# Retention attention and a mixture of experts on one core: score steps taken five at a time in place of two, and values read in another order

## The reference, cut to what matters

```python
s = jnp.einsum('bthd,bshd->bhts', q, k) * scale
logits = DEG * jnp.log(jnp.abs(s) + 1e-30) + log_G[:, :, :, None] - log_G[:, :, None, :]
logits = jnp.where(mask, logits, -jnp.inf)
m = jax.lax.stop_gradient(jnp.max(logits, axis=-1, keepdims=True))
a = jnp.exp(logits - m)
num = jnp.einsum('bhts,bshd->bthd', a, v)
den = jnp.sum(a, axis=-1).transpose(0, 2, 1)
y = num / (den[..., None] + 1e-06)      # then a norm over 64 columns, times ln_w, times w_proj
```

## Time and profile before

| | us |
|---|---|
| median of 3 runs (lowest, highest) | 1057.96 (1056.93, 1059.55) |
| the profiled execution, its own time | 1058.96 |
| its span, first to last instruction | 1056.9 |
| PE busy | 994.3 (94%) |
| DVE busy | 874.1 (83%) |
| ACT busy | 670.4 (63%) |
| POOL busy | 606.8 (57%) |

### The profile page before, as it was taken

The page is one execution under the profiler, slowest core; times in us unless marked ns, Lnnn a source line. Parts: engine busy times, 40 slices in busy tenths (PEclk is TensorE's granted clock), DMA queues, the critical chain, the costliest instruction groups (busy, mean ns, idle before and its releaser), DMA issues.

```text
span 1056.9 us, 23328 instructions
## 1 busy us (share of the span) xinstructions
PE 994.3 (94%) x8871; PEld 684.2 (65%) x8871; DVE 874.1 (83%) x1730; ACT 670.4 (63%) x1077; POOL 606.8 (57%) x593
## 2 busy tenths in 40 slices
PE   4999989999998999999999999999999999999884
PEld 2675565666665767676767676767676676767563
DVE  5678748898989998988998879898888899889972
ACT  1342445766666677777677868676878766776551
POOL 0311538888897565565756374756475666557421
PEclk9999999999999999999999999999999999999896
DMA  9301214443433353543544353545253335445530
GB/s 259 95 2 46 55 52 110 109 98 96 104 101 97 99 147 83 134 98 83 123 123 119 98 136 83 121 107 139 71 129 89 88 98 138 101 91 126 137 106 21
DMA packets 77951, 108.65 MB, mean 103 GB/s; under 512 B 15853, under 2 KB 46445, under 8 KB 77712
## 3 DMA queue, kind: packets, MB, share of 16 engines
q1 hardware_dynamic: 72768, 104.50, 38.8%
q0 software_dynamic: 5072, 2.67, 1.9%
HBM read 31.61 MB, written 11.36 MB: 41 GB/s over the span
## 4 chain that ended last, share of the span: by engine, by line
PE 74%; DVE 11%; POOL 4%; DMA 4%; issue 3%; ACT 2%; SPq 2%; POOLq 0%; DVEq 0%; ACTq 0%
PE PS L713 20%; PE PS L521 19%; PE PS L742 18%; PE PS L516 6%; PE PS L564 2%; PE PS L567 2%; PE PS L574 2%; DVE PS L1304 2%; DMA U<-H_d 2%; POOL U L1407 1%; SPq L461 1%; POOL xe_d L1439 1%; POOL Kt L1410 1%; DVE U L1271 1%; PE PS L537 1%
## 5 line engine op out<-in xcount | busy, mean ns | idle before, releaser
L713 PE MATMUL PS<-Qt,Kt 64*128 64x256 f32 (+1 forms) x2560 | 295.4, 370 | 8.1 <-DVE U L1271 7.1
L713 PEld LDWEIGHTS PS<-Qt,Kt 64*128 64x128 f32 x2560 | 219.6, 187 | 81.4 <-issue 51.7
L742 PE MATMUL PS<-U 128*64 128x256 f32 (+1 forms) x1792 | 191.6, 354 | 11.4 <-ACT U L899 11.4
L888 ACT ACTIVATE U<-PS 128x1024 f32<-128x1024 f32 x192 | 188.2, 1016 | 11.1 <-PE PS L713 8.1
L884 ACT ACTIVATE U<-U 128x768 f32<-128x768 f32 x128 | 107.7, 841 | 113.1 <-DVE U L1271 112.9
L742 PEld LDWEIGHTS PS<-U 128*64 128x64 f32 x1792 | 121.6, 138 | 87.6 <-issue 32.1
L1407 POOL TENSOR_TENSOR U<-U,consts 128x512 f32<-128x512 f32 x96 | 125.1, 1303 | 88.7 <-DMA U<-U 88.7
L1304 DVE SCALAR_TENSOR_TENSOR PS<-U,ES,PS 128x512 f32<-128x512 f32 x192 | 144.8, 754 | 17.7 <-ACT U L888 8.7
L1271 DVE SCALAR_TENSOR_TENSOR U<-PS,U 128x768 f32<-128x768 f32 x128 | 119.5, 953 | 42.6 <-PE PS L713 35.5
L1429 POOL TENSOR_SCALAR_AFFINE_SELECT U<-U 128x256 f32<-128x256 f32 x128 | 70.0, 547 | 105.4 <-ACT U L812 104.8
L1475 POOL TENSOR_TENSOR U<-U,SM 128x1024 f32<-128x1024 f32 x32 | 61.0, 1906 | 77.6 <-DVE SM L1324 77.5
(11 more groups left out here) (163 smaller groups left out, 1542.1 us busy)
## 6 DMA issues: line engine op xcount, KB each, us to landing
G<-U SPq DMA_DIRECT2D x512, 64.0 KB
U<-U SPq DMA_DIRECT2D x192, 128.0 KB, 2.4
U<-H_d SPq DMA_DIRECT2D x32, 512.0 KB
Kt<-Kt SPq DMA_DIRECT2D x32, 256.0 KB, 3.8
U<-in_w SPq DMA_DIRECT2D x21, 256.0 KB
acc<-in_x SPq DMA_DIRECT2D x4, 512.0 KB, 5.6
ye_d<-G SPq DMA_DIRECT2D x4, 512.0 KB, 8.3
U<-ye_d SPq DMA_DIRECT2D x4, 512.0 KB, 5.2
```

Of the source, the lines that this page charges most:

```text
L713: mm = te.matmul(bank[:, 256 * n:256 * n + 256 - lo], Kt[u % 2][(ki + hd) % 2][rows, 128 * j:128 * j + 128], Qt[p % 2][m // 2][rows, 256 * ...
L742: mm = te.matmul(P[4][64 * hd:64 * hd + 64, c + lo:c + 256], vt, A[s % NA][:, o:o + 256 - lo], start=i == 0 and n == 0, stop=i == m and n ...
L888: s.activation(A[n % NA], PS[:, first:first + 1024], ACT.Square, scale=0.125, bias=GUARD).then_inc(a_sq, 1)
```

## The change

PE's loop takes five steps of scores, then the side jobs due, then values; a pair is two such groups in place of five. The steps of a pair stand in a new order (`STEPS`, unit and number within it), where the off-diagonal steps of unit 1 come first. The values no longer lag a whole group: after the first five steps come four values of these same steps, after the second five the remaining six, in the order `TAKEN`. As five squares and more are alive at a time, `A` has 8 buffers in place of 4 (two of them in new memory `AX`, two in a stretch that was free). The squares of diagonal steps count on a semaphore of their own (`a_sd`), the others on `a_so`, so ACT can do them in another order (`weigh` and `square` in its table). All tables have new ticks. The experts stay at their pairs, and no arithmetic is added or taken away.

```diff
-PAIRS, NA, BATCH, HS = ((0, 1), (2, 3), (6, 7)), 4, 2, 130
+PAIRS, NA, BATCH, HS = ((0, 1), (2, 3), (6, 7)), 8, 5, 130
-PLACE_OF = (0, 1, 1, 1, 2, 2, 3, 3, 3, 3)
-FIRST_OF, END_OF = (0, 1, 4, 6), (1, 4, 6, 10)
+STEPS = ((1, 1), (1, 2), (0, 0), (1, 0), (2, 0), (2, 1), (3, 0), (3, 1), (3, 2), (3, 3))
+DIAGONAL, LATER = [STEPS.index((w, 0)) for w in range(4)], [k for k, step in enumerate(STEPS) if step[1]]
+SEARCHED = DIAGONAL[:1] + LATER
+TAKEN = (2, 0, 1, 3, 4, 5, 7, 8, 9, 6)
...
-PE_AT = [(26.84, "max", 0), (19.37, "y", 0), (25.37, "y", 1), (44.39, "fin", 0), (45.84, "fin", 1), (51.07, "wp", 0),
+PE_AT = [(31.86, "max", 0), (19.85, "y", 0), (23.54, "y", 1), (43.62, "fin", 0), (49.28, "fin", 1), (51.71, "wp", 0),
...
+ACT_AT = [(12.39, "nt", 0), (23.56, "nt", 1), (1.32, "decay", 0), (1.76, "decay", 1), (2.47, "decay", 2),
+          (8.58, "decay", 3), (19.76, "y", 0), (25.94, "y", 1), (46.98, "fin", 0), (49.72, "fin", 1),
+          (40.53, "ysq", 0), (16.61, "xe", 0), (28.7, "up", 0), (31.14, "up", 1), (36.81, "up", 2), (38.12, "up", 3),
+          (58.13, "down", 0), (-19.13, "k", 0), (-17.72, "k", 1), (-11.65, "q", 0), (-11.07, "q", 1),
+          (-17.73, "v", 0), (8.34, "v", 1), (3.78, "square", 0), (4.81, "square", 1), (12.11, "square", 2),
+          (12.93, "square", 3), (12.96, "square", 4), (16.76, "square", 5), (5.65, "weigh", 0), (6.33, "weigh", 1),
+          (10.13, "weigh", 2), (14.56, "weigh", 3)]
+DVE_AT = [(20.06, "fold", 0), (24.94, "max", 0), (51.75, "wp", 0), (51.77, "wp", 1), (26.39, "sum", 0),
+          (29.49, "var", 0), (32.96, "root", 0), (33.02, "root", 1), (35.48, "root", 2), (27.17, "up", 4),
+          (27.33, "up", 5), (31.23, "up", 6), (40.25, "up", 7), (-28.35, "k", 0), (-27.57, "k", 1), (-19.49, "q", 0),
+          (-18.17, "q", 1), (-4.35, "scale", 0), (0.03, "scale", 1), (0.04, "scale", 2), (4.18, "scale", 3),
+          (0.19, "top", 0), (0.28, "top", 1), (3.46, "top", 2), (4.8, "top", 3), (6.74, "top", 4), (6.83, "top", 5),
+          (7.08, "top", 6)]
+POOL_AT = [(63.94, "combine", 0), (79.53, "combine", 1), (86.22, "combine", 2), (-9.67, "select", 0),
+           (-9.65, "select", 1), (-7.75, "select", 2), (2.82, "select", 3), (-4.63, "vs", 1), (3.74, "vs", 2),
+           (6.22, "vs", 3), (29.14, "n1", 0), (34.55, "n2", 0), (-16.6, "k", 0), (-14.7, "k", 1), (-10.6, "q", 0),
+           (-10.57, "q", 1)]
...
+def taken_of(w, off):
+    return [n for n, k in enumerate(TAKEN) if STEPS[k][0] == w and (STEPS[k][1] or not off)]
...
-            def values(s):
+            def values(at):
+                s = at - at % 10 + TAKEN[at % 10]
...
-                if i == 0 and w % 2 == 0:
+                turns = taken_of(w, False)
+                begins, ends = at % 10 == turns[0], at % 10 == turns[-1]
+                if at % 10 in (0, 4):
...
-                        pe.wait_ge(a_nt, un // 2)
+                        pe.wait_ge(a_nt, 2 * p + w // 2)
...
+                pe.wait_ge(*squared(s))
...
-                for n in range(max(s - BATCH, 0), min(s, 320)):
+                first, last = (s, s + 4) if s % 10 == 0 else (s - 1, s + 5)
+                for n in range(first, min(last, 320)):
                     values(n)
```

More of the change, by code:

```diff
@@ L66 @@
-DVE_AT = [(27.09, "fold", 0), (28.83, "max", 0), (1.62, "scale", 0), (2.35, "scale", 1), (10.29, "scale", 4),
-          (13.78, "scale", 6), (6.3, "top", 0), (8.43, "top", 2), (12.46, "top", 3), (12.75, "top", 5),
-          (19.39, "top", 7), (19.46, "top", 8), (19.66, "top", 9), (52.68, "wp", 0), (53.61, "wp", 1),
-          (30.02, "sum", 0), (33.97, "var", 0), (39.15, "root", 0), (40.05, "root", 1), (40.62, "root", 2),
-          (52.66, "up", 4), (54.46, "up", 5), (55.33, "up", 6), (57.54, "up", 7), (-21.64, "k", 0), (-15.59, "k", 1),
-          (-20.02, "q", 0), (-9.81, "q", 1)]
@@ L107, in pair_of, with valued, searched @@
     p, k = divmod(s, 10)
-    w = PLACE_OF[k]
+    w, i = STEPS[k]
     m = ORDER[w]
-    i = k - FIRST_OF[w]
     return p, k, w, m, i, ((2 * m, 2 * m + 1) if i == 0 else (2 * i - 2, 2 * i - 1))
+def valued(s):
+    p, k = divmod(s, 10)
+    return 10 * p + TAKEN.index(k) + 1
+def searched(s):
+    p, k, w, m, i, _ = pair_of(s)
+    return 16 * p + MAXOPS[w] + (1 if m == 0 else 2 if i == 0 else 2 * i + 1)
+def taken_of(w, off):
+    return [n for n, k in enumerate(TAKEN) if STEPS[k][0] == w and (STEPS[k][1] or not off)]
 def wanted(kind, i, p):
@@ L230, in block_program @@
         Qt = [[sb(f"Qt{i}{half}", 512) for half in range(2)] for i in range(2)]
+        AX_ = sb("AX", 1024 * (NA - 6))
         NU = 25920
@@ L245, in block_program @@
         RAWq, SWPq, RAWk = (take(1024) for _ in range(3))
-        take = carve(5120)
+        take = carve(3072)
+        MORE = [take(1024) for _ in range(2)] + [AX_[:, 1024 * i:1024 * i + 1024] for i in range(NA - 6)]
         SWPk = take(1024)
@@ L249, in block_program @@
         Vt = [take(1024) for _ in range(2)]
-        A = [take(1024) for _ in range(NA)]
+        A = [take(1024) for _ in range(4)] + MORE
         RUN = [take(512) for _ in range(2)]
@@ L314, in collected, with squared @@
             return s_g[w % 2], 128 * p + 64 * (w // 2 + 1)
+        def squared(s):
+            p, k, w, _, i, _ = pair_of(s)
+            return (a_sd, 4 * p + w + 1) if i == 0 else (a_so, 6 * p + sum(n > 0 for _, n in STEPS[:k + 1]))
         def read_out(job):
@@ L320, in read_out @@
                 p, k, w, m, at, _ = pair_of(i)
-                return (v_t, 4 * p + w + 1) if at == 0 else (a_sq, i + 1)
+                return (v_t, 4 * p + w + 1) if at == 0 else squared(i)
             if kind == "q":
@@ L456, in rows @@
                 sp.wait_ge(s_zy, 64)
[L457 removed]
+                sp.wait_ge(v_mx, 16 * p + MAXOPS[w + 1])
                 if p:
@@ L742, in values @@
                         mm = te.matmul(P[4][64 * hd:64 * hd + 64, c + lo:c + 256], vt, A[s % NA][:, o:o + 256 - lo],
-                                       start=i == 0 and n == 0, stop=i == m and n == 1)
+                                       start=begins and n == 0, stop=ends and n == 1)
                 mm.then_inc(p_av, 1)
@@ L883, in square @@
                     ac.wait_ge(v_t, 4 * p + w + 1)
-                    s.activation(a_, a_, ACT.Square).then_inc(a_sq, 1)
+                    s.activation(a_, a_, ACT.Square).then_inc(a_sd, 1)
                 else:
@@ L900, in _ @@
                 elif kind == "square":
-                    square(10 * p + i)
+                    square(10 * p + LATER[i])
+                elif kind == "weigh":
+                    square(10 * p + DIAGONAL[i])
                 elif kind == "decay":
@@ L1355, in _ @@
                 if kind == "scale":
-                    diagonal(10 * p + i)
+                    diagonal(10 * p + DIAGONAL[i])
                 elif kind == "top":
-                    maximum(10 * p + i)
+                    maximum(10 * p + SEARCHED[i])
                 elif kind == "fold":
```

47 lines of the change are left out of this document (17 added, 30 removed), and 6 rows, old and new, of the table PE_AT.

## The result

The changed kernel takes 1051.35 us (median of 5 runs, 1050.11 to 1053.0), the one before, on the same chip, 1058.45 (5 runs, 1056.93 to 1060.0). The ratio is 0.9933, interval 0.9917 to 0.995: a gain of 7.1 us, under one per cent, where 31.5 were forecast, and outside the range of 1010 to 1047. The profiled execution took 1052.39, its span is 1050.3.

A forecast was written before the change was run, and what follows sets the result against it. PE was taken as the bound, with DVE close behind. Gains of 9.2 (plain windows), 15.1 (expert windows), 4.8 (pairs 2 to 7), 2 (start) and 3.4 (end), less 3 for banks, made 31.5 us: from 1058.96 to 1027, range 1010 to 1047.

The forecast's parts named there:

- The other lists: Reordered engine lists: cost PE nothing within its pace; two plain pairs take 50.4 us, 2.3 less than before.
- The end: Pairs 30 and 31: DVE's additions come later and its last maximum earlier; gain 3.4 us.
- Two groups in place of five: PE's loop: three cycles of shape changes a pair go, 0.36 us each, 34.6 us of PE time.
- banks: Five score steps share three pairs of banks: waits of 0 to 19 us in all, 3 us taken.
- Rival C: Emptying of banks: each group waits 0.3 us for a bank, giving 1043 us; chance 0.17.
- Rival E: PE's excess belongs to each step, not each cycle of shape changes, giving 1055 us; chance 0.05.
- Values behind longer groups: PE's values: the copy of bank 4 is asked for later, so its 11.4 us of waits go.
- Pairs 2 to 7: Early pairs, POOL's scattering on top of the loop: gain of nothing to 3.3 us a window, 4.8 in all.
- rival D: Query rotations on POOL starved behind the first scaling: slower, 1070 us if DVE is 2.4 us late; chance 0.06.
- Pairs 0 and 1: First pairs, which wait for the start as well: gain of 2 us.
- A: The main forecast as summed: 1027 us, between 1018 and 1038; chance 0.62.
- B: PE stays the bound everywhere, so all switches and the listed waits go: about 1006 us; chance 0.10.

The follow-up runs named there:

- E11: E2 with POOL's first scaling done for half its columns and six of DVE's maximum operations a pair halved (work left out); 1028.68 us.
- E4: The kernel before, with a product of 8 columns in the scores' shape ahead of each of the 64 query products; 1071.33 us, ratio 1.0135.
- E15: E12 with DVE's first maximum of unit 3 reading PSUM in place of one SBUF input (masked square left out); 1035.18 us.
- E14: E2 with DVE's first maximum of unit 3 reading PSUM in place of one SBUF input (masked square left out); 1043.42 us.
- E12: E2 with six of DVE's maximum operations a pair taking half their columns, POOL's first scaling whole; 1039.73 us, ratio 0.9805.
- E2: The changed kernel with loads and additions of the experts' results moved later, behind pair 31's rows and maskings; 1043.21 us, ratio 0.9876.
- E10: E2 without 55 of the 58 token scatters that POOL issues during the pairs (work left out); 1028.1 us, ratio 0.971.
- E13: E11 with E10's scatters left out as well, all three reliefs together; 1013.72 us, ratio 0.9559.
- E1: The changed kernel with the next pair's query rotations ahead of the first scaling on POOL's list; 1088.49 us, ratio 1.0306.
- E5: E2 with POOL's scatters in two clumps, three before the second scaling and five behind it, not spread evenly; 1060.2 us, ratio 1.0019.
- E6: E2 with the transposes of the maxima earlier, ahead of the second group's scores, as a block of their own; 1099.37 us, ratio 1.0396.
- E9: E6 with DVE's reduction of the maxima ahead of the fourth masking; 1048.48 us, ratio 0.9931.
- E8: E2 with POOL's first scaling done for half of its columns (work left out); 1036.25 us, ratio 0.9795.

## Why the prediction was wrong

The step that failed is "The other lists", which let every engine but PE follow within PE's pace or a few tenths of a us behind it. It missed 11.3 us in pairs 2 to 7 (POOL's list) and 7.7 in pairs 8 to 29 (two limits of one length, and a pace read from the wrong pairs). "The end" failed in the same way, by 9.1 us (SP's queue and DVE's additions). The steps on PE's own time held.

**Two groups in place of five, and banks: right.** Forecast 0.36 us a cycle less 0.05 for banks, 0.31. Where PE isn't held up, six pairs (14 to 19) have a busy PE for 166.91 us before and 161.23 in E11: 5.7 for 18 cycles, 0.32 each. E4 gave 0.33 for a cycle added. The banks' share shows in the first group of a pair, 4.05 us in place of 3.9: its fifth step begins 0.17 us late, where the forecast had it arrive together with the end of the second square. That is 5 us over 32 pairs, near the 3 taken and far from the 19 of the upper end. Rival C is out. The busy time of the scores fell from 295.4 to 281.6 us and that of the values from 286.7 to 280.0, with unchanged counts, as the forecast wanted, if 20 us are "some tens". Rival E is out too: two expert pairs went from 58.1 to 56.4 us.

**Values behind longer groups: right.** The wait of 11.4 us is gone, and none for squares took its place but 1.0 us in four pieces (L545 for ACT) and one piece of 2.0 us in pairs 0 and 1.

**The other lists: wrong, and it is the main step.** The forecast took the larger of DVE's 49.9 and the loop's 50.1, added 0.3, and had 50.4 us for two plain pairs (the loop's own terms, 24.5 and 25.4, make 49.9 and not 50.1); 51.25 were measured (25.31 and 25.94, pairs 14 and 19). Two expert pairs (15 and 16) were as forecast: 28.65 + 27.70 = 56.35, near 56, PE without idle time. For the plain ones three things failed.
First a term: the scaling was taken as 1.90 us; on the loop it takes 2.29, as an operation of DVE now runs beside it. Twice 0.39 is the 0.8 us missing, and E15, without it, has 50.4. But E15 has DVE's list shortened as well: with the whole list E14's two plain pairs take 25.79 + 26.44 = 52.2 us, so the term alone doesn't explain the miss.
Second, two limits of one length don't act as the larger one: with DVE's cut the port alone gives 3.1 us (E12 to E15), without it nothing (E2 to E14). The room that one relief makes in a pair is taken in the next, where the other engine is late. In all, DVE and the loop took 6.6 us from pairs 8 to 29 (after against E11), of the 7.7 missed.
Third, I read the two-pair windows as plain and expert ones. But pair 14 took 23.80 before, and pair 15, in the same window, 28.89. The plain pairs of the old order, 14 and 19, took 23.80 + 27.63 = 51.4 together, hardly more than after. There was little to gain in them: 0.2 us, where I had put 2.3. In the forecast's own windows, the four called plain (8, 14, 20 and 26) got 6.5 us longer in place of 9.2 shorter, and the other seven 21.0 shorter in place of 15.1; a part of this is side work that the new ticks moved between windows.

**Pairs 2 to 7: wrong, and my bound was wrong too.** I let the scatters bring the gain down to nothing at worst, and there was a loss of 6.5 us. POOL was busy for 47.79 of 53.74 us, and I took that as room; but scaling and rotations, 7.6 us (543.09 to 550.71), now stand on the loop in one piece, and scatters that stand ahead of it on POOL's list make it late. POOL's timeline of the changed kernel shows it:

```profile
228.43 1.27 POOL L1471 DMA_INDIRECT xe_d<-U,idx_s  x1 [0.17 <-issue]
230.00 0.97 POOL L1471 DMA_INDIRECT xe_d<-U,idx_s  x1 [0.30 <-issue]
...
241.19 1.27 POOL L1471 DMA_INDIRECT xe_d<-U,idx_s  x1 [0.15 <-issue]
242.50 1.91 POOL L1507 TENSOR_TENSOR U<-U,SM 128x1024 f32<-128x1024 f32 x1
```

There is no idle time ahead of the scaling: the list came late, not DVE; pair 4 began at 249.75, after 2.57 us of waiting. In the pair before POOL had waited 4.3 us for the same scaling. So in one pair the loop was late and in the next POOL's list. One reading behind this bound was off as well: PE's slices weren't at nine tenths from slice 8 on, but at eight tenths in slice 12, 317 to 343 us, in pairs 6 and 7, where before already had waits. E10 takes 155.2, near the 156.8 of the forecast. This is rival D's place, the rotations behind the scaling. Its sign, a wait of over 1 us, came in plain pairs too (1.60 us ahead of pair 14), but its cause did not: DVE reached the reduction in time and waited 0.19 us there for PE's transposes (541.74), and ahead of pair 4 it was POOL's own list that was late.

**The end: wrong.** I counted DVE's additions, and not the queue on which their loads stand. SP had the loads ahead of the rows that the maxima need, and the additions came ahead of pair 31's maskings: +5.7 us where -3.4 was forecast. E2 gives -2.3, and the tail after pair 31 as worked out.

**Pairs 0 and 1** gained 4.3 us, 2 were taken. As this stretch ends at 192.3 us in E15 and at 196.1 in E12, which hardly differ in it, the size of that gain isn't well known.

**What that makes of A.** E15 has the end repaired, no port conflict and a shorter list of DVE; less the 10.9 us that E10 gained in pairs 2 to 7 it would take about 1024 (an estimate from two runs), near A's 1027. E10 lies there too, with 1028.1. As each of these kernels leaves work out, neither is support for A's sum. E13, 1013.7, lies between A and B. What stays open: DVE and POOL were only made lighter by leaving work out, and no order was found that has both loops short; E1, E5, E6 and E9 each moved the loss somewhere else. Why E8 and E12 gain 3 us at the end wasn't followed up.

## What to carry to other kernels

When a bound is taken away, work out the closed loop over all engines for each stage, and take each duration from a place where the same neighbours run, or ask what the new neighbour reads; if the next two limits lie within a few per cent, count on neither relief alone and on less than the difference. A side engine's busy share is no room once its work stands on the loop in one piece: ask what is queued ahead of it, and in what order the queue that feeds it goes, the transfers' too. Let the range of a stage reach into a loss wherever its chain gets longer, even if every engine gets less to do. And a number in a list of ticks means another place in another table: look where the moved items came to stand before reading the result.
